# Row maxima of the diagonal blocks in 384 instead of 512 columns, with two small transfers that put the shared part in place

## The reference

```
q = (x @ Wq).reshape(B, S, 2 * H, d).transpose(0, 2, 1, 3) * scaling
k = (x @ Wk).reshape(B, S, 2 * H, d).transpose(0, 2, 1, 3)
scores = jnp.einsum('bhqd,bhkd->bhqk', q, k)
scores = jnp.where(causal_mask, -jnp.inf, scores)
probs = jax.nn.softmax(scores, axis=-1)
...
attn_weights = probs[:, :, 0] - lam * probs[:, :, 1]
attn = jnp.einsum('bhqk,bhkd->bhqd', attn_weights, v)
```

## Time and profile before

| what | before |
|---|---|
| time, median of 3 runs | 432.58 us (432.31 to 432.9) |
| time of the profiled execution | 432.0 us |
| its span | 430.3 us |
| granted PE clock over the span | 0.958 |
| instructions | 16520 |

### The profile page before, as it was taken

One profiled execution on the slowest core, in us unless ns is written; L12 is line 12 of the kernel. 1 busy time (PEld: TensorE's weight loads), 2 busy tenths in 40 slices (PEclk: granted clock), 3 DMA queues, 4 the chain that ended last, 5 costly groups with the idle time before them and its releaser, 6 DMA issues.

```text
span 430.3 us, 16520 instructions
## 1 busy us (share of the span) xinstructions
PE 391.2 (91%) x5697; PEld 188.0 (44%) x5697; DVE 394.6 (92%) x551; ACT 349.5 (81%) x731; POOL 236.4 (55%) x574
## 2 busy tenths in 40 slices
PE   4846899999999999999999999999999999998882
PEld 3512344444444444444444444444444444444462
DVE  1889899999999999999999999999999999894585
ACT  2521799999999999999999999999999999986444
POOL 7300132666666666666666666666666666669432
PEclk9975599999999999999999999999999999999897
DMA  5465254311111111111111111111111110100002
GB/s 144 175 218 169 77 199 151 100 53 51 52 54 50 50 50 50 50 50 50 50 50 50 50 50 50 50 50 50 50 50 50 50 51 27 30 1 2 2 24 73
DMA packets 21389, 28.42 MB, mean 66 GB/s; under 512 B 4960, under 2 KB 9952, under 8 KB 21232
## 3 DMA queue, kind: packets, MB, share of 16 engines
q1 hardware_dynamic: 20768, 27.58, 21.2%
q10 hardware_dynamic: 592, 0.46, 0.4%
HBM read 20.39 MB, written 9.47 MB: 69 GB/s over the span
## 4 chain that ended last, share of the span: by engine, by line
PE 63%; ACT 17%; DVE 6%; issue 6%; POOL 3%; DMA 2%; SPq 1%; ACTq 1%; DVEq 0%; POOLq 0%
PE acc L689 29%; ACT e_buf L1032 15%; PE mx L607 13%; PE ex L659 10%; DVE part_max L1135 4%; PE ex L697 3%; PE ex L643 2%; PE mx L616 1%; SPq L319 1%; DMA x_tok<-in_L_attn_x 1%; PE mx L823 1%; PE mx L781 1%; ACT o_rows L959 1%; DMA km<-k_rows 1%; PE ex L708 1%
## 5 line engine op out<-in xcount | busy, mean ns | idle before, releaser
L1135 DVE TENSOR_REDUCE part_max<-mx 128x2 f32<-128x1024 f32 (+2 forms) x288 | 338.7, 1219 | 5.6 <-PE mx L607 1.6
L1032 ACT ACTIVATE e_buf<-ex 128x512 f32<-128x512 f32 x576 | 304.5, 602 | 33.8 <-PE ex L659 33.0
L689 PE MATMUL acc<-e_buf,v_grp 128*32 128x256 f32 x2756 | 181.5, 352 | 4.1 <-issue 1.9
L533 POOL TENSOR_SCALAR_AFFINE_SELECT e_buf<-e_buf 128x256 f32<-128x256 f32 x256 | 100.1, 409 | 151.7 <-ACT e_buf L1032 151.7
L659 PE MATMUL ex<-qe,ke 26*128 26x512 bf16 (+3 forms) x768 | 148.7, 335 | 0.4 <-ACT e_buf L1032 0.3
L607 PE MATMUL mx<-km,qm 29*128 29x128 bf16 (+3 forms) x1280 | 117.0, 270 | 10.7 <-DVE part_max L1135 8.7
L607 PEld LDWEIGHTS mx<-km,qm 26*128 26x128 bf16 (+1 forms) x1280 | 41.8, 94 | 110.2 <-issue 66.5
L689 PEld LDWEIGHTS acc<-e_buf,v_grp 128*32 128x32 f32 x2756 | 64.9, 109 | 55.9 <-issue 45.3
L659 PEld LDWEIGHTS ex<-qe,ke 26*128 26x128 bf16 x768 | 46.8, 91 | 21.2 <-ACT e_buf L1032 10.8
L516 POOL TENSOR_TENSOR r_rms<-sq_eps,minus_half 128x16 f32<-128x16 f32 x15 | 43.7, 2912 | 0.0
L616 PE MATMUL mx<-mask,pick 32*128 32x128 bf16 x512 | 25.9, 220 | 0.0
(11 more groups left out here) (139 smaller groups left out, 259.4 us busy)
## 6 DMA issues: line engine op xcount, KB each, us to landing
qm<-q_rows SPq DMA_DIRECT2D x32, 128.0 KB, 2.5
km<-k_rows SPq DMA_DIRECT2D x32, 128.0 KB, 2.7
qe<-q_rows SPq DMA_DIRECT2D x32, 128.0 KB, 2.5
ke<-k_rows SPq DMA_DIRECT2D x32, 128.0 KB, 2.7
q_rows<-part_q SPq DMA_DIRECT2D x6, 256.0 KB, 2.8
k_rows<-part_k SPq DMA_DIRECT2D x6, 256.0 KB, 3.0
q_rows<-part_q SPq DMA_DIRECT2D x6, 192.0 KB
k_rows<-part_k SPq DMA_DIRECT2D x6, 192.0 KB
```

Source lines behind the costliest of these rows:

```text
L533: pool.affine_select(out=e, in_=e, compare_op=ALU.is_ge, fill=0.0, base=0, pattern=[[0, PAIR], [1, P]], channel_multiplier=-1)\
L689: last = pe.matmul(out, v, e, start=first, stop=over, skip_group_check=True)
L1032: nc.scalar.activation(e_buf[:, b, i, :], ex[:, ex_slot(b, i) % EX_BANKS, :], ACT.Exp).then_inc(s["exped"], 1)
L1135: nc.vector.tensor_reduce(target, mx_of(n, pr, m)[:].rearrange("p s (a b) -> p s a b", a=a), AX.X, ALU.max).then_inc(s["maxed"], 1)
```

## The change

Of a diagonal block, the queries 0 to 63 need only the keys 0 to 63. So a diagonal unit becomes six segments of 64 columns instead of eight. Segments 0 to 3 are the keys 0 to 63 of its four blocks, for all 128 queries. The keys 64 to 127 matter only to queries 64 to 127: segments 4 and 5 each hold two blocks. Blocks 0 and 1 of the unit put theirs in PSUM partitions 64 to 127, where these queries are; blocks 2 and 3 use the free partitions 0 to 63. DVE reduces 2 x 384 instead of 2 x 512 columns, to six maxima a map. The two high ones go by transfer (`move_high`) to their place, partitions 64 to 127 and slot 4 (`HIGH_SLOT`) of their block, so that `part_max` has five slots a block. `combine` waits for these transfers and reduces five slots instead of four. On PE a diagonal unit now takes 24 matmuls instead of 16: eight with 64 columns, eight with 64 weight columns and 64 columns, and eight for the mask, of which four have 6 x 32 and four 2 x 32 columns.

```diff
 MAX_UNITS = [
-    ([(P * i, i, i, 1) for i in range(4)], True, (4, 0, 4)),
-    ([(P * i, 4 + i, 4 + i, 1) for i in range(4)], True, (4, 16, 4)),
...
+    (0, None),
+    (1, None),
...
-        part_max = [sb(f"part_max{i}", [P, PAIR, NB * MSLOTS]) for i in range(2)]
+        part_max = [sb(f"part_max{i}", [P, PAIR, HALVES, SLOTS, ENTRIES]) for i in range(2)]
...
+        def move_high(sp, n, pr):
+
+            wait(sp, s["maxed"], NU * n + 2)
+            for e in range(2):
+                rows = part_max[pr][BLOCK * (1 - e):BLOCK * (2 - e)].rearrange("p j h i e -> p (j h) i e")
+                own = part_max[pr][BLOCK:P].rearrange("p j h i e -> p (j h) i e")
+                sp.dma_start(own[:, :, HIGH_SLOT, 2 * e:2 * e + 2], rows[:, :, 0, 4:ENTRIES]).then_inc(s_high[pr], 16)
...
             write_parts(sp, 0, slice(HEAD, P), s["rows_b0"])
+            move_high(sp, 0, 0)
             load_exp_rows(sp, 1, 1)
             load_max_rows(sp, 2, 0)
+            move_high(sp, 1, 1)
             place_maxima(sp, 0, 0, 0)
...
                     load_max_rows(sp, n + 3, 1 - pr)
+                if not isinstance(n, int) or n + 2 < NPAIR:
+                    move_high(sp, n + 2, pr)
                 if not isinstance(n, int) or n + 1 < NPAIR:
                     place_maxima(sp, n + 1, 1 - pr, g + pr)
...
+            def diagonal_unit(pr, bank, h):
+
+                for r in range(4):
+                    t = P * (4 * h + r)
                     for jj in range(PAIR):
                         j = PAIR + jj
-                        rows = slice(STRIP * j, STRIP * j + used)
-                        last = pe.matmul(bank[:, jj, col:col + P * nk], qm[pr][rows, P * qb:P * (qb + 1)],
-                                         km[pr][rows, P * kb:P * (kb + nk)], start=i == 0,
-                                         stop=not masked and i == len(matmuls) - 1, skip_group_check=True)
-                for c in range(4 if masked else 0):
+                        rows = slice(STRIP * j, STRIP * j + ROWS)
+                        pe.matmul(bank[:, jj, BLOCK * r:BLOCK * (r + 1)], qm[pr][rows, t:t + P],
+                                  km[pr][rows, t:t + BLOCK], start=r == 0, stop=False, skip_group_check=True)
+                for r in range(4):
+                    t = P * (4 * h + r) + BLOCK
+                    col = BLOCK * (4 + r % 2)
+                    own = slice(0, BLOCK) if r >= 2 else slice(BLOCK, P)
+                    for jj in range(PAIR):
+                        j = PAIR + jj
+                        rows = slice(STRIP * j, STRIP * j + ROWS)
+                        pe.matmul(bank[own, jj, col:col + BLOCK], qm[pr][rows, t:t + BLOCK],
+                                  km[pr][rows, t:t + BLOCK], start=False, stop=False, skip_group_check=True)
+                for c in range(4):
+                    first = 0 if c < 2 else 4
...
+                        own = slice(STRIP * (c % 2), STRIP * (c % 2 + 1))
+                        cols = mask[rows, 0, 0:STRIP].unsqueeze(1).broadcast_to([STRIP, ENTRIES - first, STRIP])
...
-            def combine(n, par):
+            def combine(n, par, visit):
 
                 dve.wait_ge(s["maxed"], NU * (n + 1))
...
+                wait(dve, s_high[par], 32 * (visit + 1))
+                blocks = part_max[par][:].rearrange("p j h i e -> p (j h) e i")[:, :, 0:4, :]
```

More of the change, by code:

```diff
@@ L596, in max_unit @@
                 n = 2 * g + pr
-                matmuls, masked, _ = MAX_UNITS[m]
-                used = ROWS if masked else COARSE
+                matmuls, _ = MAX_UNITS[m]
                 if m == 0:
@@ L602, in max_unit @@
                 bank = mx_of(n, pr, m)
-                for i, (col, qb, kb, nk) in enumerate(matmuls):
+                if isinstance(matmuls, int):
+                    last = diagonal_unit(pr, bank, matmuls)
+                else:
+                    for i, (col, qb, kb, nk) in enumerate(matmuls):
+                        for jj in range(PAIR):
+                            j = PAIR + jj
+                            rows = slice(STRIP * j, STRIP * j + COARSE)
+                            last = pe.matmul(bank[:, jj, col:col + P * nk], qm[pr][rows, P * qb:P * (qb + 1)],
+                                             km[pr][rows, P * kb:P * (kb + nk)], start=i == 0,
+                                             stop=i == len(matmuls) - 1, skip_group_check=True)
@@ L604, in max_unit @@
+                last.then_inc(s["max_scored"], 1)
+            def diagonal_unit(pr, bank, h):
+                for r in range(4):
+                    t = P * (4 * h + r)
                     for jj in range(PAIR):
                         j = PAIR + jj
[L606 to L609 removed]
@@ L613, in max_unit @@
                         rows = slice(STRIP * j, STRIP * (j + 1))
[L614 to L617, removed]
+                        own = slice(STRIP * (c % 2), STRIP * (c % 2 + 1))
+                        cols = mask[rows, 0, 0:STRIP].unsqueeze(1).broadcast_to([STRIP, ENTRIES - first, STRIP])
+                        out = bank[:, jj, BLOCK * first:BLOCK * ENTRIES].rearrange("p (a t) -> p a t", t=BLOCK)
+                        last = pe.matmul(out[:, :, own], pick[rows, c, :], cols, start=False, stop=c == 3,
                                          skip_group_check=True)
-                last.then_inc(s["max_scored"], 1)
+                return last
             def place_free(n, at):
@@ L1129, in max_unit @@
                 n = 2 * g + pr
-                _, _, (a, at, step) = MAX_UNITS[m]
+                matmuls, target = MAX_UNITS[m]
                 dve.wait_ge(s["max_scored"], NU * n + m + 1)
@@ L1159, in _ @@
             late = {0: [(low, 6)], 1: [(low, 7)],
-                    NU: [(combine, 0, 0)], NU + 1: [(split_low, 0)]}
+                    NU: [(combine, 0, 0, 0)], NU + 1: [(split_low, 0)]}
             for u in range(NU + EARLY):
@@ L1178, in burst @@
                 if m == NU:
-                    combine(n + 1, 1 - pr)
+                    combine(n + 1, 1 - pr, g + pr)
                 if m == NU + 1:
```

39 lines of the change are left out of this document (31 added, 8 removed), and 7 rows, old and new, of the table MAX_UNITS.

## The result

| what | before | after |
|---|---|---|
| time, median | 432.5 us | 438.5 us (438.0 to 439.98) |
| time of the profiled execution | 432.0 us | 438.0 us |
| its span | 430.3 us | 436.3 us |
| granted PE clock over the span | 0.958 | 0.956 |
| instructions | 16520 | 17664 |

What follows compares the result with a forecast made beforehand. The prediction took PE's own work to bound the kernel, not DVE. Burst 3's 6.4 us plus 1.0 us at the start gave 7.4 on the profiled 432.0, so 439.4, median 440.0 us, range 433 to 449.

Steps and rivals of the forecast that it cites:

- DVE's part: DVE's shorter diagonal reduces, less two longer combines, save 0.50 us a pair; counted as zero because DVE waits for PE.
- PE's part: Burst 3's diagonal unit: two changes of matmul kind at 0.10 plus 0.02 for scores, 0.22 us; 29 pairs give 6.4 us.
- burst 4's unit is hidden: The second diagonal unit's 0.22 us stays behind ACT's copy and exponentials, so nothing of it comes through.
- The start: From 24 to 50 us, at low PE clock with DVE setting the pace: 1.0 us slower, bounds -0.8 and 2.5.
- `combine` of pair 0 now waits for two transfers: At the start, transfers queued behind SP's row writes land at 37.0 to 37.8 us, `combine` due near 36.9: 0.5 us.
- The 1.5 us for PE at the low clock: At the start, costlier diagonal units on PE: 0.4 at the first, 0.3 at pair 1's first, 0.8 in pair 0's bursts.
- DVE's -0.8: At the start, where DVE sets the pace, three of the four shorter reduces give 0.8 us back.
- The margin of 1.0 us: SP has both extra issues out by 214.8 us, `place_maxima` follows at 215.8: 1.0 us left, cost zero.
- SP would be late: Rival: slow issues of 8-byte pieces, from 1.1 us each, make SP set the beat; 446 to 452 us, chance 0.07.
- DVE as the pace: Rival: PE fills units only as DVE frees buffers, so every pair loses 0.50 us; 417.6 us, chance 0.05.
- small matmuls at full price: Rival: twos of 64 columns cost as much as 128, 0.45 in burst 3, 0.17 in burst 4; 452 us, chance 0.12.
- no price for the 64-column kind: Rival: changing to 64-column matmuls in diagonal units costs PE nothing; 432 to 433.3 us, no measurable change, chance 0.13.

Runs made afterwards that it cites:

- the other order: Changed kernel with the eight matmuls of 64 weight columns put first in each diagonal unit, ahead of the eight of 128: 436.7 us, ratio 1.0079.
- changed, shifted, one unit packed: Changed kernel, diagonal units one place later (bursts 4 and 5), the first in its old 512-column form, only the second packed: 436.2 us, ratio 1.0078.
- wide: Changed kernel with the eight matmuls of each diagonal unit's last 64 keys made 128 weight columns wide: 432.9 us, ratio 1.0005.
- changed, shifted: Changed kernel with both packed units moved one place later (bursts 4 and 5), and the transfers of the high maxima one unit later: 437.0 us.
- 64 columns first, shifted: Changed kernel with diagonal units one place later and the matmuls of 64 weight columns first in each: 434.5 us, ratio 1.0015.
- before, shifted, with transfers: Kernel before with diagonal units one place later, plus two small transfers a pair that nobody reads and DVE's wait for them: 429.1 us, ratio 0.9915.
- before, shifted: Kernel before with its two old 512-column diagonal units moved one place later, to bursts 4 and 5: 429.5 us, ratio 0.9906.

## Why the prediction was right, and where it was off

**DVE's part, counted as zero.** Right, and shown: DVE's gain alone moved the step by 0.009 us and the time by nothing that can be measured. The argument was that DVE had 0.05 us to wait at each unit and PE's unit was 0.9 us clear of it; the busy share of 92% said the opposite and misled. One small size was off: each combine was to grow by 0.02 us and grew by 0.07 (starts 0.13 apart before, 0.20 after; 209 ns became 289). It cost nothing for the same reason.

**PE's part.** The mechanism was right, and the run with eight wider matmuls shows it together with the run with the other order: two holes of 0.09 to 0.10 us, no cost of the small matmuls. In burst 3 the term was 0.22 us and the timeline shows 0.19 to 0.20. That the price of 0.10 fitted so well is partly luck: it came from rows with other kinds, and the reading of the earlier trace rows takes 0.11 us for the stream of the second transpose, where the two transposes start 0.17 us apart (205.05 and 205.22); with that the gap to the products would be 0.03, not 0.09. The step shows 0.157, less than the timeline, since a part came back in another place, by the small transfers ahead of the placing of the maxima: 0.023 us by the run without them (11.032 - 10.852 = 0.180 for the packing alone), 0.043 by the run that added them to the kernel before. The prediction had counted them as zero. So the pairs cost 29 x 0.157 = 4.6 us where 6.4 were forecast: the mis-sized term. That burst 4's unit is hidden was right, shown by the two runs with one unit packed.

**The start.** Forecast +1.0 us, measured -0.5 at the third combine and -0.1 at the fourth. The step that failed is "`combine` of pair 0 now waits for two transfers": these were issued from 33.63 us on, and with 1.9 us to landing the second (issued from about 34.4) was there by 36.3, before the combine, which started at 36.6 with no wait. The prediction had taken 2.5 us to landing, from transfers of 128 KB; those of 2 KB take 1.9. The 1.5 us for PE at the low clock was too much as well: DVE's -0.8 and the measured -0.5 leave 0.3 for it up to the third combine, and about 0.6 one pair on. Which part of it was wrong was not separated.

**The end.** 1.4 us came behind the last combine, and no term stood for it. In before the granted clock is 0.61 from 397 to 401 us and 1.00 from 404 to 408; in the changed kernel it is 0.60 and 0.57: a second low stretch. Windows of the changed kernel (columns as in the earlier trace rows):

```profile
397.00:401.00 4.00, 4.00 (x32) 2.32 (x27) 1.64 (x4) 1.08 (x2) 4.00 (x5) 0.60 0.00 0
...
404.00:408.00 4.00, 3.90 (x38) 1.48 (x41) 1.57 (x7) 2.27 (x6) 1.29 (x4) 0.57 0.00 0
```

Near 0.6 and 0.57 most of the stretch is at the lower level, 1.2 GHz. All 14 traces say that this is where the 1.4 us lies: the time from the start of the last combine to the end of the span goes with the mean granted clock of 388 to 409 us, and not with the form of the units.

| mean granted clock, 388 to 409 us | traces | us behind the last combine |
|---|---|---|
| 1.00 | before with transfers; changed, shifted, one unit packed | 55.9, 56.0 |
| 0.92 | before; wide; changed, shifted; 64 columns first | 56.3, 56.2, 56.1, 56.5 |
| 0.84 | changed; without transfers; 64 columns first, shifted; before, shifted, with transfers | 57.7, 57.7, 57.5, 57.7 |
| 0.76 | only burst 4 packed; only burst 3 packed; before with 384 columns for DVE; before, shifted | 58.1, 58.1, 58.1, 58.3 |

Every row of the table has kernels with old units and kernels with packed ones, so no run ties the low stretches to the change; what sets their number and length is open. The sum 4.6 + 0.5 - 0.5 + 1.4 = 6.0 is the measured one; the forecast's 7.4 had one term 1.8 too high, one 1.0 too high, and lacked 1.4. That the first two and the third partly cancel is luck.

**SP and the rivals.** The margin of 1.0 us was forecast and is 1.02; an issue of 8-byte pieces takes 0.66 us in the median (two of the 64 took 1.44), far from the 1.1 at which SP would be late, and taking the transfers away brought nothing. DVE as the pace, small matmuls at full price and no price for the 64-column kind are each excluded by a run or a row.

## What to carry to other kernels

Count the kinds of matmul, not only their columns: on this chip a quarter fewer columns for DVE cost two changes of kind, 0.20 us, on PE, and PE was what the pairs waited for. Ask of the engine to be relieved whether anything waits for it, and of the engine that takes on the work in which burst it has time; moving the old units by one burst gave 0.9%, more than any packed kernel gained. Judge such edits by the step of the loop first, which one trace gives to 0.005 us here, and then ask whether the total follows: low stretches of the clock near the end made its last part 0.2 to 2.4 us longer here.

## What the runs showed of the hardware that was not expected

- A change between matmuls of 64 and of 128 weight columns, in the same 32 rows, cost 0.09 to 0.10 us each time, in either direction. Between the changes the narrow ones are no slower: eight of 64 weight columns need 0.07 us from first to last start, as against 0.10 for eight of 128 weight columns.
- DVE's small reduces grew from 209 to 289 ns for 16 elements more and another layout, 5 ns an element, where the large ones cost 1.05.
- With two small transfers ahead of it, the placing of the maxima was there 0.03 us earlier after its issue, and the step was shorter by 0.02 to 0.04 us (0.01 in the shifted kernel), even where nothing uses what they move.
- Low stretches of the granted clock near the end made the same last part of the program 55.9 to 58.3 us long.
